# A mixture-of-experts stage: all weights loaded once, feed-forward halves in a software pipeline, and the routing search between them

## The reference, cut to what matters

```python
def _L0_ffn_ref(x, router_w, w1, b1, w2, b2):       # x: 4 x 1024 x 128
    E = 8                                            # HIDDEN = 512
    capacity = max(1, int(Sz * 2.0 / E) + 1)         # 257
    scores = softmax(einsum('bsd,ed->bse', x, router_w), axis=-1)
    gate_vals, sel_idx = top_k(swapaxes(scores, 1, 2), capacity)
    tokens = x[b_idx, sel_idx]
    h = gelu(einsum('becd,edh->bech', tokens, w1) + b1)      # exact gelu
    y = einsum('bech,ehd->becd', h, w2) + b2
    return zeros_like(x).at[b_idx, sel_idx].add(y * gate_vals[..., None])
```

## Time and profile before

| what | value |
|---|---|
| median of 3 runs | 6354.95 us (6347.94 to 6364.27) |
| profiled execution, first to last instruction (span) | 6365.1 us |
| time of the profiled execution besides its span | not given by the profile |
| TensorE matmuls busy | 5238.0 us (82%) |
| TensorE weight loads busy | 3186.2 us (50%) |
| VectorE busy | 4208.1 us (66%) |
| ScalarE busy | 2952.3 us (46%) |
| GpSimd busy | 2688.6 us (42%) |
| mean granted TensorE clock | 0.914 of full speed |

### The profile page before, as it was taken

How to read it: one execution, slowest core, us unless ns; L and a number is a source line. 1 busy time by engine, 2 the same in 40 slices (tenths; PEclk the granted TensorE clock), 3 DMA queues, 4 the chain that set the end, 5 groups by cost and what they waited for, 6 DMA issues and landing times. The chain is left out here.

```text
span 6365.1 us, 149552 instructions
## 1 busy us (share of the span) xinstructions
PE 5238.0 (82%) x55030; PEld 3186.2 (50%) x55030; DVE 4208.1 (66%) x5662; ACT 2952.3 (46%) x4796; POOL 2688.6 (42%) x1428
## 2 busy tenths in 40 slices
PE   4745777638888898589999999999899899999996
PEld 3633445412323222156666666666666666666664
DVE  4354111234343444489999888988898889899995
ACT  0001222213333333256666666666666666666663
POOL 0000000020000000277777777777677676767772
PEclk8756889859898999799999999999999999999997
DMA  0000110031101000111112111211211121111111
GB/s 19 0 8 8 30 30 22 22 55 23 20 10 20 10 11 1 39 48 38 37 34 61 35 36 37 58 36 34 60 35 36 35 57 38 33 38 42 35 36 48
DMA packets 154627, 202.75 MB, mean 32 GB/s; under 512 B 42073, under 2 KB 80867, under 8 KB 152815
## 3 DMA queue, kind: packets, MB, share of 16 engines
q1 hardware_dynamic: 154512, 201.17, 13.5%
HBM read 63.67 MB, written 11.53 MB: 12 GB/s over the span
## 5 line engine op out<-in xcount | busy, mean ns | idle before, releaser
L1772 POOL TENSOR_TENSOR d_rnorm<-d_sq_clip,neg_half 128x32 f32<-128x32 f32 x192 | 1048.5, 5461 | 67.0 <-DVE d_sq_clip L1604 66.4
L1762 POOL TENSOR_TENSOR d_qk_swap<-d_qk_raw,d_rot 128x512 f32<-128x512 f32 x768 | 960.1, 1283 | 16.5 <-ACT d_qk_raw L1447 15.3
L931 DVE TENSOR_REDUCE c_mx<-c_ps 128x1 f32<-128x512 f32 (+3 forms) x768 | 422.5, 557 | 710.7 <-PE c_ps L810 704.6
L1221 PE MATMUL d_pair<-d_wqkv,d_xin 128*128 (+1 forms) x1536 | 752.7, 614 | 91.6 <-DVE d_probs L1625 38.8
L99 POOL TENSOR_TENSOR ln_post_rstd<-ln_post_var,neg_half 128x8 f32<-128x8 f32 x16 | 26.6, 1661 | 1831.7 <-DVE ln_post_var L80 1831.7
L909 ACT ACTIVATE c_pt<-c_ps 128x512 f32<-128x512 f32 (+1 forms) x640 | 353.8, 554 | 712.8 <-PE c_ps L825 711.1
L839 PE MATMUL c_ps<-c_pt,c_vg 128*32 128x512 f32 (+3 forms) x1536 | 627.8, 505 | 4.1 <-DVE c_ots L936 4.1
L1749 POOL TENSOR_TENSOR d_probs<-d_probs,d_prec 128x1024 f32<-128x1024 f32 x192 | 369.0, 1922 | 466.6 <-DVE d_prec L1636 466.6
L1233 PE MATMUL d_pair<-ident,d_qk_part 128*128 128x128 f32 x3072 | 431.5, 280 | 142.2 <-DVE d_qk_part L1615 139.2
L1233 PEld LDWEIGHTS d_pair<-ident,d_qk_part 128*128 128x128 f32 x3072 | 359.8, 143 | 325.1 <-issue 242.1
L1586 DVE TENSOR_TENSOR d_qk_part<-d_qk_raw,d_rot 128x1024 f32<-128x1024 f32 x384 | 471.8, 1229 | 47.6 <-issue 34.2
(11 more groups left out here) (248 smaller groups left out, 9687.5 us busy)
## 6 DMA issues: line engine op xcount, KB each, us to landing
d_band<-d_own_t SPq DMA_DIRECT2D x768, 64.0 KB, 2.0
d_band<-d_prev_t SPq DMA_DIRECT2D x576, 64.0 KB, 2.0
d_v_prev<-d_v SPq DMA_DIRECT2D x192, 128.0 KB, 2.3
b_w<-in_L_ffn_w SPq DMA_DIRECT2D x64, 256.0 KB, 3.5
d_band_prev<-d_prev_t SPq DMA_DIRECT2D x192, 64.0 KB, 2.0
d_wqkv<-in_L_ffn_Wqkv SPq DMA_DIRECT2D x6, 1536.0 KB, 8.8
c_qp<-c_q_scratch SPq DMA_DIRECT2D x96, 64.0 KB
c_kp<-c_k_scratch SPq DMA_DIRECT2D x96, 64.0 KB
```

What stands on the lines that cost most here:

```text
L931: eng.tensor_reduce(mx[:, hh, qt, k0 // 512:k0 // 512 + 1], ps[:, S1B[c % 2], 0:nk], AX.X, ALU.max).then_inc(mx_done, 1)
L1221: eng.matmul(bank(QK_AT[u][c]), xin[p][:, :], wqkv[:, bass.ds(par, 1), c * 512:(c + 1) * 512].rearrange("p l n -> p (l n)"), start=True, s ...
L1762: mm = eng.tensor_tensor(qk_swap[:, which, :, out:out + hd], qk_raw[:, which, :, src:src + hd], rot[:, bass.ds(par, 1), which, 1, bass.ds( ...
L1772: eng.tensor_tensor(rnorm[:, :], sq_clip[:, :], neg_half[:, 0:2 * HEADS], ALU.pow).then_inc(rn_ready, 1)
```

## The change

The experts stage alone changes.

- All experts' w1, b1, w2 and b2 are loaded once, into tiles that hold all eight experts, by eleven DMAs at the start of the stage. Every engine that uses them waits for all eleven.
- The staging tile xin goes: TensorE transposes straight from y_all, four tiles into one PSUM bank, and ScalarE and VectorE take turns in copying a bank to xt. GpSimd sets y_all to zero after the last transpose.
- The four first-layer matmuls of the next half are issued ahead of the sixteen second-layer matmuls of this one, across experts and sequences too.
- ScalarE copies each half's result from py into one of 16 ring places; VectorE works on the ring. ScalarE waits for VectorE's count `gated` when the ring is full.
- The 31 counts of the search are issued by TensorE between the matmuls of the first sequence's halves, three in each step; the two ranking matmuls come after step 11. The scores and the ranks now use the bank pm[1].
- The first and the last sequence are written out; a loop takes the two between them.

The diff, cut to its core:

```diff
-        def pairs(eng, step):
-            with eng.Fori(0, BATCH) as b:
-                with eng.Fori(0, E // 2) as pair:
-                    for u in range(2):
-                        step(b, pair * 2 + u, b * E + pair * 2 + u, u, b * (E // 2) + pair)
+        def halves(step):
+            for i in range(HALVES):
+                step(0, i, i)
+        def later_halves(eng, step):
+            with eng.Fori(1, BATCH - 1) as b:
+                for i in range(HALVES):
+                    step(b, i, b * HALVES + i)
+            for i in range(HALVES):
+                step(BATCH - 1, i, (BATCH - 1) * HALVES + i)
...
             @block.sync
-                    eng.wait_ge(expert_used, n * 2)
-                    eng.dma_start(w1[u][:, :], dram["L0_ffn_w1"][one].rearrange("e d h -> (e d) h")).then_inc(w_in[u], 16)
...
+                eng.dma_start(w1[:, :, :], dram["L0_ffn_w1"].rearrange("e d h -> d e h")).then_inc(w_in, 16)
+                eng.dma_start(b1[:, :, :], dram["b_b1"].rearrange("e p c -> p e c")).then_inc(w_in, 16)
+                for e in range(E):
+                    eng.dma_start(w2[:, e, :, :], dram["L0_ffn_w2"][e].rearrange("(c p) d -> p c d", p=P)).then_inc(w_in, 16)
+                eng.dma_start(b2[:].rearrange("p e d -> p (e d)"), dram["L0_ffn_b2"].rearrange("e d -> (e d)").partition_broadcast(P)).then_inc(w_in, 16)
+                eng.wait_ge(w_in, 16 * W_DMAS)
             @block.gpsimd
+                eng.wait_ge(turned, GROUPS)
+                eng.memset(y_all[:], 0.0)
+                eng.drain().then_inc(zeroed, 1)
             @block.tensor
+                for g in range(GROUPS):
+                    if g >= 4:
+                        eng.wait_ge((xt_act, xt_dve)[g % 2], g // 2 - 1)
+                    for t in range(4):
+                        mm = eng.transpose(ph[g % 4][:, t * P:(t + 1) * P], y_all[:, 4 * g + t, :], ident[:, :])
+                    mm.then_inc(turned, 1)
...
+                eng.wait_ge(w_in, 16 * W_DMAS)
+                def counted(k):
+                    eng.wait_ge(count_ready, k + 1)
+                    eng.matmul(pm[0][:, 0:BATCH * E], ones[:, :], count[:, :], start=True, stop=True).then_inc(total_ready, 1)
+                def widened(b, i, n, c):
+                    half, e = i % 2, i // 2
+                    if not (isinstance(n, int) and n == 0):
+                        eng.wait_ge(gelu_done, 4 * n + c - 3)
...
+                    eng.matmul(ph[c][:, :], w1[:, e, c * P:(c + 1) * P], cols, start=True, stop=True).then_inc(h_done, 1)
+                def narrowed(i, n, lo, hi):
+                    e = i // 2
+                    if lo == 0:
+                        eng.wait_ge(gelu_done, 4 * n + 4)
+                        if not (isinstance(n, int) and n < 2):
+                            eng.wait_ge(copied, n - 1)
+                    for t in range(lo, hi):
                         for c in range(HC):
+                            mm = eng.matmul(py[i % 2][:, t, :], ht[i % 2][:, c, t * P:(t + 1) * P], w2[:, e, c, :],
+                                            start=(t == 0 and c == 0), stop=(c == HC - 1), skip_group_check=True)
+                    if hi == 4:
                         mm.then_inc(y_done, 1)
+                def step(b, i, n):
+                    routing = isinstance(n, int) and n < HALVES
+                    last = isinstance(n, int) and n == N - 1
+                    after = (b, i + 1, n + 1) if i + 1 < HALVES else (b + 1, 0, n + 1)
+                    if not last:
+                        for c in range(HC - 1):
+                            widened(*after, c)
+                    if routing and 3 * n < 31:
+                        counted(3 * n)
+                    if not last:
+                        widened(*after, HC - 1)
+                    narrowed(i, n, 0, 2)
+                    if routing and 3 * n + 1 < 31:
+                        counted(3 * n + 1)
+                    narrowed(i, n, 2, 4)
+                    if routing and 3 * n + 2 < 31:
+                        counted(3 * n + 2)
+                    if routing and n == 31 // 3 + 1:
+                        ranked()
+                for c in range(HC):
+                    widened(0, 0, 0, c)
+                halves(step)
+                later_halves(eng, step)
             @block.scalar
...
+                def step(b, i, n):
+                    if not (isinstance(n, int) and n == N - 1):
+                        curved((i + 1) % HALVES, n + 1)
+                    eng.wait_ge(y_done, n + 1)
+                    if not (isinstance(n, int) and n < RING):
+                        eng.wait_ge(gated, n - RING + 1)
+                    eng.activation(ring[:, i % RING, :, :], py[i % 2][:], ACT.Copy).then_inc(copied, 1)
             @block.vector
...
-                eng.memset(y_all[:], 0.0)
-                eng.drain()
+                eng.wait_ge(zeroed, 1)
+                eng.wait_ge(w_in, 16 * W_DMAS)
...
+                    part = ring[:, i % RING, :, :]
+                    eng.wait_ge(copied, n + 1)
+                    eng.tensor_tensor(part, part, b2[:, e:e + 1, :].broadcast_to((P, 4, D)), ALU.add)
```

More of the change, by code:

```diff
@@ L360, in experts_stage @@
         gates = sb("gates", [P, BATCH * E, TB])
[L361 to L364, removed]
+        w1 = sb("w1", [P, E, HID])
+        w2 = sb("w2", [P, E, HC, D])
+        b1 = sb("b1", [P, E, HC])
+        b2 = sb("b2", [P, E, D])
         ht = [sb(f"ht{k}", [P, HC, 512]) for k in range(2)]
-        part = sb("part", [P, TB, D])
+        ring = sb("ring", [P, RING, 4, D])
         ph = [ctx.enter_context(nc.psum_tensor(f"b_ph{k}", [P, 512], F32)) for k in range(4)]
@@ L414, in _ @@
                 eng.wait_ge(c_in, 32)
[L415 to L422, removed]
+                for g in range(GROUPS):
[4 more added lines that the diff above has]
+                    mm.then_inc(turned, 1)
                 for n in range(NT):
-                    mm = eng.matmul(ph[0][:, n * E:(n + 1) * E], xt[:, n * P:(n + 1) * P], router[:, :], start=True, stop=True,
+                    if n % 4 == 0:
+                        eng.wait_ge((xt_act, xt_dve)[(n // 4) % 2], n // 8 + 1)
+                    mm = eng.matmul(pm[1][:, n * E:(n + 1) * E], xt[:, n * P:(n + 1) * P], router[:, :], start=True, stop=True,
                                     skip_group_check=True)
@@ L434, in _ @@
[L434 to L442, removed]
-                        for c in range(HC):
[L444 to L453, removed]
-                        mm.then_inc(y_done, 1)
@@ L456, in _, with ranked @@
-                pairs(eng, step)
+                def ranked():
+                    eng.wait_ge(eq_ready, 1)
+                    flat = equal[:].rearrange("p a t -> p (a t)")
+                    eng.matmul(pm[1][:, 0:NT * E], before[:, :], flat, start=True, stop=True, skip_group_check=True)
+                    eng.matmul(pm[1][:, NT * E:2 * NT * E], ones[:, :], flat, start=True, stop=True, skip_group_check=True).then_inc(rank_ready, 1)
+                def widened(b, i, n, c):
+                    half, e = i % 2, i // 2
+                    if not (isinstance(n, int) and n == 0):
+                        eng.wait_ge(gelu_done, 4 * n + c - 3)
+                    at = b * SEQ + half * 512
+                    cols = xt[:, at:at + 512] if isinstance(b, int) else xt[:, bass.ds(at, 512)]
+                    eng.matmul(ph[c][:, :], w1[:, e, c * P:(c + 1) * P], cols, start=True, stop=True).then_inc(h_done, 1)
@@ L458, in _ @@
+                for c in range(HC):
+                    widened(0, 0, 0, c)
+                halves(step)
+                later_halves(eng, step)
             @block.scalar
             def _(eng):
[L460 to L464, removed]
+                for g in range(0, GROUPS, 2):
+                    eng.wait_ge(turned, g + 1)
+                    eng.activation(xt[:, g * 512:(g + 1) * 512], ph[g % 4][:, :], ACT.Copy).then_inc(xt_act, 1)
@@ L469, in _, with curved @@
                 eng.activation(score[:], score[:], ACT.Exp).then_inc(exp_ready, 1)
[L471 to L480, removed]
+                eng.wait_ge(w_in, 16 * W_DMAS)
+                def curved(i, n):
+                    e = i // 2
+                    for c in range(HC):
+                        eng.wait_ge(h_done, 4 * n + c + 1)
+                        eng.activation(ht[i % 2][:, c, :], ph[c][:, :], ACT.Gelu, bias=b1[:, e, c:c + 1]).then_inc(gelu_done, 1)
+                def step(b, i, n):
[5 more added lines that the diff above has]
+                    eng.activation(ring[:, i % RING, :, :], py[i % 2][:], ACT.Copy).then_inc(copied, 1)
+                curved(0, 0)
+                halves(step)
+                later_halves(eng, step)
             @block.vector
             def _(eng):
[L484 to L488, removed]
+                for g in range(1, GROUPS, 2):
+                    eng.wait_ge(turned, g + 1)
```

(1 more changed line is left out.)

65 lines of the change are left out of this document (29 added, 36 removed).

## The result

The changed kernel takes 6017.59 us (median of 4 runs, 6012.99 to 6019.35); the kernel before, beside it, 6356.65 us (4 runs, 6347.94 to 6364.27). The ratio is 0.9468, 95% interval 0.9454 to 0.9481: 339 us less, where the forecast was 329 less and 6026. The span of the profiled execution is 6017.0 us, its mean granted clock 0.931.

The account below looks back on a forecast made before the run. TensorE, its waits and its clock were taken to bound the experts stage. Start at 450.0, search steps and 7.05 us halves summed to a stage end of 921.2 instead of 1250.5, 329 less: 6026 us, range 6006 to 6084.

Parts of the forecast that it names:

- first W starts: Start of the first half's four first-layer matmuls, after router scores and weight loads: 450.0 us, bounds 443 and 453.
- first W and three chunks: First half's four first-layer matmuls, cold, 6.28 us to 456.3, then three of the next half's four, to 458.9.
- ten search steps: First ten steps over halves, three threshold-search counts in each: 8.34 us per step, bounds 7.7 and 9.3, together 83.4.
- Part 1: Transposes and router scores: 32 transposes take 7.8 us, scores 13.82, ending at 449.4 us instead of 461.3.
- Part 2: Expert weights as one 4.73 MB batch: in between 443 and 453 us; all 15 later waits, 125.2 us, go.
- rival of late weights: Biases in 16-byte pieces, queued behind the 2 MB load, delay the first-layer matmuls to near 465: 6041 us; chance 0.12.
- sign that TensorE waits once for weights: In the experts stage, TensorE's wait for weights appears once if the forecast is right.
- Part 3: TensorE issues the next half's first-layer matmuls before this half's second-layer ones: 0.85 us gelu wait goes, 7.05 us per half.
- Part 4: Threshold search under the halves, three counts a step: slots 2.86, 2.70 (TensorE waits about 0.7) and 2.78, 8.34 us.
- rival of the falling clock: TensorE's stops in the search drop its clock to 1.2 GHz: 15.0 us a step instead of 8.34, 6093; chance 0.10.
- rival that the pipeline buys nothing: Second-layer matmuls still wait for a gelu, as first-layer ones wait for bank-freeing gelus: 54.8 us stay, 6081; chance 0.05.
- slower case: Unbroken TensorE stretch is granted only 1.2 GHz, 13.7 us per half; with all halves so, 6445; chance 0.03.

## Why the prediction was right, by its own steps

The sum was off by 6.9 us at the end of the stage, 914.3 against 921.2. Term by term:

| step | forecast | measured |
|---|---|---|
| first W starts | 450.0 | 444.6 |
| first W and three chunks | 8.9 | 8.87 |
| ten search steps | 83.4 (8.34 each) | 84.3 (8.43 each) |
| rest of step 10, step 11, ranking | 12.6 | 12.53 |
| step 12 to the end of the stage | 366.3 (7.05 a half) | 363.96 (7.01) |
| stage saved | 329 | 336.3 |

**Part 1 was mis-sized.** Thirty-two transposes took 6.4 us and not 7.8, the scores 11 us and not 13.82. Both were costed at the clock of 0.50 that the rows showed, and nothing in the sum allowed for another. Issued back to back, the transposes brought the clock up near their end (0.59 from 431.0, 1.00 from 433.6), and the first scores profited before it fell to 0.50 again. Of the 1.4 us at the transposes some 1.0 are an error of the sum, not the clock: four times 1.95 counts the modelled end of a group four times, while at 0.50 the transposes start some 0.21 us apart (17 in 3.60 us from 427.4), 6.8 us for 32. The early start is 5.4 of the 6.9 us.

**Part 2 held.** The bounds for the weights, 443 and 453, contain the 444.29 that was measured where nothing else bound. In that kernel the 4.73 MB took 18.3 us from the first issue of a weight load, at 425.95, to the start of W. The Trainium skill's fixed 2.0 us plus bytes at 436 GB/s (DMA: Bandwidth & Descriptors, "Anatomy of one DMA") would have had 440 by my estimate; the page gives that fit for one DMA issued by GpSimd, and here SyncE issued eleven, so this is no test of the page. The rival of late weights, near 465, did not come about: the biases in 16-byte pieces landed after 8.9 us, with the 2 MB load ahead of them. But the weights were the later of the two in the second profile of the changed kernel, by 0.46 us, and I had let the scores alone set the start. The sign that TensorE waits once for weights held in that profile and not in the first.

**Part 3 held to 0.04 us a half.** I had taken 7.05 as the mean of 7.00, from back-to-back work of another stage, and 7.11 from this one. The unbroken cadence was the right row: with no wait ahead, N does take 3.57 and not 3.67.

**Part 4 held.** I had one slot with a wait, 2.70, and two without, 2.86 and 2.78; measured 2.67, 2.86 and 2.91, the last because there the weight load of the count waits for VectorE (until 461.77 in the first step, 2.77 us after the count before). The rival of the falling clock is refuted by 1.00 from 453.5 to 538, with stops of 0.5 us. What the Trainium skill describes (TensorE: Matmul & The Clock Gate, "A second HAM failure mode") did not happen here.

**The rival that the pipeline buys nothing** is refuted by the kernel that put the order back. Its price came out by luck: I took the counted 54.8 us of 64 halves, and 55.5 were measured in the stage, but as 53 halves at 1.04, since the wait hardly shows in the search steps. **The slower case** needed a low clock in the long stretch; it was 1.00.

The profiled span fell by 348, not 336; the difference lies in the last stage (from its first load to the end of the span 3693.8 us before, 3680.3 after), whose length varies between the ten profiles of the same code, 3675 to 3722, and the medians say 339. That 12 us of this scatter fell on the faster side is luck: my forecast of the span, 6036, missed 6017.0 by 19, of which the stage explains 7.

## What to carry to other kernels

Cost a removed wait by the period around it, not by the counted idle time: here the restarts at the lower clock made 165 us of a counted 125, and the modelled end of a matmul and a weight load that could not be made ahead made 1.04 us a half of a listed 0.78. When a serial search on one engine is laid under the matrix work of another, put as much work between two of its rounds as one round takes; where less stands between, the matrix engine waits for the remainder. A buffer ring bought nothing where its consumer was never late; look at what the consumer does in the meantime before giving it space.

## What the runs showed of the hardware that I had not expected

Transposes alone, issued back to back, raised the granted clock. In the kernel without the pipeline, TensorE did nothing but transposes from 427.37 to about 432.9:

```profile
427.40:430.00 2.60, 2.60 (x13) 2.60 (x14) 0.62 (x1) 0.60 (x1) 0.00 (x0) 0.50 0.85 265
430.00:431.50 1.50, 1.50 (x9) 1.50 (x9) 0.48 (x2) 0.60 (x1) 0.00 (x0) 0.50 1.05 390
431.50:432.80 1.30, 1.30 (x13) 1.30 (x12) 0.81 (x2) 0.70 (x2) 0.00 (x0) 0.98 1.01 386
432.90:438.00 5.10, 5.10 (x49) 5.10 (x47) 0.75 (x2) 0.40 (x1) 3.51 (x1) 1.00 1.18 283
```

The clock was 0.50 at first, 0.98 from 431.5 and 1.00 behind them. The Trainium skill (TensorE: Matmul & The Clock Gate, "Part 4: PE-mode transpose") says that the higher level doesn't engage for transposes; this trace disagrees. When it rose differed between executions of the same instructions (1.00 only from 433.6 in the changed kernel), and the time from the first transpose to the end of the scores was 14.3 us in one and 17.4 us in the other. Of the eight profiles with these instructions four took some 14.3 us and four some 17.4. The scores themselves, with 8 columns each, let it fall again to 0.50 while they were still running.
